# Cross-attention output projection in three fp32r products, with a single load buffer for the rows and a merge ahead

## The reference

```python
attn = jnp.einsum('bhts,bshk->bthk', probs, v)
out = jnp.einsum('bthk,hkd->btd', attn, Wo) + bo      # Wo: (16, 64, 512)
...
x = x + _L0_xattn_ref(_layernorm(x, axis=-1), ctx_1024, ctx_1024, ...)
```

## Time and profile before

| | |
|---|---|
| three timed runs | 3259.77, 3262.93, 3263.29 us (median 3262.93) |
| profiled execution | 3259.59 us, its span 3257.8 us |
| mean granted TensorE clock | 0.94 |
| busy: PE, VectorE, ScalarE, GpSimd | 3059.9, 1683.3, 1445.1, 115.1 us |
| L896, projection, 128 records | 592 ns each; overlapped |
| L886, bias row, 16 records | 7.8 us busy |
| L934, merge, 8 | 1.22 us each |
| L55, addition of two halves, 8 | 2.35 us each |
| DMA traffic | 253.18 MB, mean 78 GB/s |

### The profile page before, as it was taken

The page is one execution under the profiler, slowest core; times in us unless marked ns, Lnnn a source line. Parts: engine busy times, 40 slices in busy tenths (PEclk is TensorE's granted clock), DMA queues, the critical chain, the costliest instruction groups (busy, mean ns, idle before and its releaser), DMA issues. The chain is left out here.

```text
span 3257.8 us, 61769 instructions
## 1 busy us (share of the span) xinstructions
PE 3059.9 (94%) x25814; PEld 2672.7 (82%) x25814; DVE 1683.3 (52%) x2786; ACT 1445.1 (44%) x2978; POOL 115.1 (4%) x87
## 2 busy tenths in 40 slices
PE   6899999999999999999999999999989789969997
PEld 5788888888888888888888888888746689959997
DVE  5355655565565556556565655656533765530001
ACT  3355555555555555555555555555532420011111
POOL 0000000000000000000000000000040320100000
PEclk9799999999999999999999999999999855579998
DMA  7311221121122112112211211211270000217661
GB/s 310 110 51 39 75 65 44 44 75 52 39 75 65 45 47 77 46 39 77 63 45 56 78 39 48 78 41 41 51 172 1 17 33 0 96 56 282 251 227 60
DMA packets 234822, 253.18 MB, mean 78 GB/s; under 512 B 22328, under 2 KB 169944, under 8 KB 234096
## 3 DMA queue, kind: packets, MB, share of 16 engines
q1 hardware_dynamic: 233040, 241.79, 23.2%
q0 software_dynamic: 1280, 4.20, 0.4%
q10 hardware_dynamic: 288, 4.19, 0.3%
HBM read 215.42 MB, written 34.70 MB: 77 GB/s over the span
## 5 line engine op out<-in xcount | busy, mean ns | idle before, releaser
L272 PE MATMUL fills<-wv_group,ctxT_hi 128*128 128x256 f32 x4096 | 777.1, 285 | 1.3 <-DVE ctxT_lo L477 0.6
L280 PE MATMUL fills<-ctxT_hi,wk_pairs 128*128 128x512 f32 x2048 | 703.9, 405 | 0.6 <-DVE keys L492 0.6
L272 PEld LDWEIGHTS fills<-wv_group,ctxT_hi 128*128 128x128 f32 x4096 | 644.6, 189 | 24.2 <-issue 20.3
L492 DVE SCALAR_TENSOR_TENSOR keys<-fills,bk,keys 64x512 fp32r<-64x512 f32 x512 | 383.8, 750 | 407.5 <-ACT keys L409 403.8
L272 PE MATMUL fills<-wv_group,ctxT_lo 128*128 128x256 f32 x2048 | 571.9, 279 | 0.0
L409 ACT ACTIVATE keys<-fills,bk 64x512 fp32r<-64x512 f32 x512 | 349.5, 683 | 404.4 <-PE fills L280 401.1
L280 PEld LDWEIGHTS fills<-ctxT_hi,wk_pairs 128*128 128x128 f32 x2048 | 385.6, 188 | 102.9 <-issue 23.9
L280 PE MATMUL fills<-ctxT_lo,wk_pairs 128*128 128x512 f32 x1024 | 401.3, 392 | 0.0
L485 DVE TENSOR_TENSOR values<-fills,values 128x512 fp32r<-128x512 f32 x256 | 176.6, 690 | 416.7 <-ACT values L404 416.7
L272 PEld LDWEIGHTS fills<-wv_group,ctxT_lo 128*128 128x128 f32 x2048 | 387.0, 189 | 0.0
L529 DVE TENSOR_TENSOR probsT<-probsT_ps,probsT 128x512 fp32r<-128x512 f32 x504 | 348.2, 691 | 67.4 <-ACT probsT L441 58.8
(11 more groups left out here) (210 smaller groups left out, 2999.4 us busy)
## 6 DMA issues: line engine op xcount, KB each, us to landing
e_w<-in_L_ffn_W SPq DMA_DIRECT2D x64, 1024.0 KB, 8.8
ctx_stage<-in_ctx SPq DMA_DIRECT2D x128, 256.0 KB, 2.9
wv_group<-wv_split SPq DMA_DIRECT2D x64, 512.0 KB, 4.7
wk_pairs<-wk_split SPq DMA_DIRECT2D x128, 256.0 KB, 3.3
q<-q_split SPq DMA_DIRECT2D x256, 64.0 KB, 2.7
q_split<-p_qb SPq DMA_DIRECT2D x16, 512.0 KB, 3.8
o_parts<-o_half SPq DMA_DIRECT2D x128, 64.0 KB, 1.9
a_ua<-o_parts SPq DMA_DIRECT2D x32, 256.0 KB, 5.4
```

The costliest lines, as they stand in the source:

```text
L272: last = nc.tensor.matmul(pJ[:, bank[0], 256 * k:256 * k + 256], c[:, t, s:s + P], wv[:, w, t, :], start=t + n == 0, stop=t == DT - 1 and ...
L280: last = nc.tensor.matmul(pJ[:, bank[0], :], wk[:, p, w, t, :], c[:, t, 512 * j:512 * j + 512], start=t + n == 0, stop=t == DT - 1 and n == 2)
L492: last = nc.vector.scalar_tensor_tensor(out=keys[lo_rows(j), x, 512 * j:512 * j + 512], in0=pJ[DK * a:DK * a + DK, bk_, :], scalar=bk_sb[h ...
```

## The change

- Wo is split in two fp32r tiles, `a_xo_hi` and `a_xo_lo`, the second in place of `a_xo`. ScalarE copies the first part in four pieces, one ahead of each of its four steps of head 13 of the last batch; GpSimd subtracts the second in one instruction, between its additions of batches 0 and 1.
- Room for it: `a_ua` holds one batch instead of two, `a_w` two weights instead of three. SP loads batch 0 ahead of head 12's stores, batch 1 at head 13 after the addition of batch 0, batch 2 at head 14 after the addition of batch 1, each following one after the addition of the batch before it. The third weight is loaded in the projection block, after batch 3.
- The merged rows `a_oT`, fp32, lie in two buffers in memory of the later tile `s_AT`. ScalarE copies their first part (fp32r), VectorE subtracts the second (`rest`, both operands in SBUF). The value bias is split likewise.
- PE makes 24 fp32r products a batch instead of 16 fp32 records, and 24 for the bias row.
- VectorE's order is: rest b, merge b+1, residual b-1. ScalarE's is: widen 0 and 1, then for each b the copy of batch b, widen b+2, and after b = 0, 2 and 5 a weight copy. GpSimd's weights come after b = 1 and 5.

```diff
-        self.w = at("a_w", [P, 3, DT, D], 4096)
-        self.ua = at("a_ua", [P, 2, 2, XH // 2, P], 10240)
+        self.xo_lo = at("a_xo_lo", [P, XH // 2, D], 0, F32R)
+        self.xo_hi = at("a_xo_hi", [P, XH // 2, D], 4096, F32R)
+        self.w = at("a_w", [P, 2, DT, D], 8192)
+        self.ua = at("a_ua", [P, 2, XH // 2, P], 12288)
...
     def add(self, nc, pool, b):
-        pool.wait_ge(self.u_in[b % 2], 64 * (b // 2 + 1))
+        pool.wait_ge(self.u_in, 64 * (b + 1))
...
-                    for n in range(2):
-                        early.u_load(sp, o_parts, n)
+                    early.u_load(sp, o_parts, 0)
...
-                    for n in range(3):
-                        sp.dma_start(early.w[:, n, :, :], aw[n].rearrange("(t p) d -> p t d", p=P)).then_inc(early.w_in, 16)
-                if i >= 2:
-                    sp.wait_ge(early.added, i - 1)
+                    for n in range(2):
+                        early.w_load(sp, aw, n)
+                if i in (1, 2):
+                    sp.wait_ge(early.added, i)
...
-            for b in range(2):
-                early.add(nc, pool, b)
+            early.add(nc, pool, 0)
+            pool.wait_ge(early.xo_split, 4)
+            nc.gpsimd.tensor_tensor(early.xo_lo[:, :, :], early.xo[:, :, :], early.xo_hi[:, :, :].bitcast(F32),
+                                    ALU.subtract).then_inc(early.xo_rest, 1)
+            early.add(nc, pool, 1)
...
+                            if not more and i == 1:
+                                act.wait_ge(early.xo_in, 16)
+                                nc.scalar.copy(early.xo_hi[:, 2 * j:2 * j + 2, :], early.xo[:, 2 * j:2 * j + 2, :]
+                                               ).then_inc(early.xo_split, 1)
...
-                    for b in range(4, B):
-
-                        sp.wait_ge(early.added, b - 1)
+                    for b in range(3, B):
+
+                        sp.wait_ge(early.added, b)
                         early.u_load(sp, o_parts, b)
+                        if b == 3:
+                            sp.wait_ge(w_lo, 1)
+                            early.w_load(sp, aw, 2)
...
                         for a in range(XH // 2):
-                            last = nc.tensor.matmul(pY[:, b % 2, :], oT[:, b % 2, a, :], early.xo[:, a, :],
-                                                    start=a == 0, stop=a == XH // 2 - 1)
+                            for k, (m, w) in enumerate(((0, early.xo_hi), (0, early.xo_lo), (1, early.xo_hi))):
+                                last = nc.tensor.matmul(pY[:, b % 2, :], oT_p[:, b % 2, m, a, :], w[:, a, :],
+                                                        start=a + k == 0, stop=a == XH // 2 - 1 and k == 2)
...
-                        if b in (1, 3):
-                            weights_lo((b + 1) // 2)
+                        if b in (1, 5):
+                            weights_lo(1 + b // 4)
...
+                    def rest(b):
+                        dve.wait_ge(oT_hi, b + 1)
+                        if b >= 2:
+                            dve.wait_ge(projected, b - 1)
+                        nc.vector.tensor_tensor(oT_p[:, b % 2, 1, :, :], oT[:, b % 2, :, :], oT_p[:, b % 2, 0, :, :].bitcast(F32),
+                                                ALU.subtract).then_inc(oT_lo, 1)
...
+                    merge(0)
+                    for b in range(B):
+                        rest(b)
+                        if b + 1 < B:
+                            merge(b + 1)
...
+                    widen(0)
+                    widen(1)
+                    for b in range(B):
+                        act.wait_ge(merged, b + 1)
+                        if b >= 2:
+                            act.wait_ge(projected, b - 1)
+                        nc.scalar.copy(oT_p[:, b % 2, 0, :, :], oT[:, b % 2, :, :]).then_inc(oT_hi, 1)
+                        if b + 2 < B:
+                            widen(b + 2)
+                        if b in (0, 2, 5):
+                            n = b // 2
+                            act.wait_ge(early.w_in[n % 2], 16 * (n // 2) + 16)
+                            nc.scalar.copy(w_p[:, n, 0, :, :], early.w[:, n % 2, :, :]).then_inc(w_hi, 1)
```

More of the change, by code:

```diff
@@ L42, in __init__ @@
         self.xbv = left("a_xbv", [P, XH // 2])
-        self.xo_in, self.rs_in, self.w_in, self.added = (sem(n) for n in ("a_xo_in", "a_rs_in", "a_w_in", "a_added"))
-        self.u_in = [sem("a_u_in0"), sem("a_u_in1")]
+        self.xo_in, self.xbv_in, self.rs_in, self.added = (sem(n) for n in ("a_xo_in", "a_xbv_in", "a_rs_in", "a_added"))
+        self.xo_split, self.xo_rest, self.u_in = sem("a_xo_split"), sem("a_xo_rest"), sem("a_u_in")
+        self.w_in = [sem("a_w_in0"), sem("a_w_in1")]
     def u_load(self, sp, o_parts, b):
@@ L794, with self_attention @@
 ITERS = 20
[L797 removed]
+def self_attention(nc, x, x_bo, o_parts, row_scale, early, shared_space, aw, bq, bk, bv, wo, bo, ident, x1, route, wg, b1, b2, buf,
                    weights, first_weights, used):
@@ L835, in self_attention @@
             with ExitStack() as s1:
-                oT = sb("a_oT", [P, 2, XH // 2, P], F32, s1)
+                oT = AT[:, 0:XH, :].rearrange("p (b a) t -> p b a t", b=2)
+                oT_p = sb("a_oTp", [P, 2, 2, XH // 2, P], F32R, s1)
+                xbv_p = sb("a_xbvp", [P, 2, XH // 2], F32R, s1)
                 rsx = sb("a_rsx", [P, XH // 2, P], F32, s1)
@@ L928, in residual, with merge @@
                         norm_steps(nc, dve, step, x1, stats, mv, b)
-                    for b in range(B):
+                    def rest(b):
[4 more added lines that the diff above has]
+                                                ALU.subtract).then_inc(oT_lo, 1)
+                    dve.wait_ge(xbv_hi, 1)
+                    nc.vector.tensor_tensor(xbv_p[:, 1, :], early.xbv[:, :], xbv_p[:, 0, :].bitcast(F32),
+                                            ALU.subtract).then_inc(xbv_lo, 1)
+                    def merge(b):
                         dve.wait_ge(early.added, b + 1)
@@ L950, in _, with widen @@
                 def _(act):
-                    for b in range(B):
+                    def widen(b):
                         act.wait_ge(early.rs_in, 16 if b < B - 1 else 32)
@@ L956, in _ @@
                                        early.rs[:, b, :].unsqueeze(2).to_broadcast([P, XH, DK])).then_inc(widened, 1)
-                        if b in (0, 2, 4):
-                            act.wait_ge(early.w_in, 48)
-                            nc.scalar.copy(w_p[:, b // 2, 0, :, :], early.w[:, b // 2, :, :]).then_inc(w_hi, 1)
+                    act.wait_ge(early.xbv_in, 16)
+                    nc.scalar.copy(xbv_p[:, 0, :], early.xbv[:, :]).then_inc(xbv_hi, 1)
+                    widen(0)
[11 more added lines that the diff above has]
+                            nc.scalar.copy(w_p[:, n, 0, :, :], early.w[:, n % 2, :, :]).then_inc(w_hi, 1)
                     act.wait_ge(var_ready, 1)
```

26 lines of the change are left out of this document (15 added, 11 removed).

## The result

The changed kernel is slower: 3280.8 us at the median (3278.9 to 3282.1), the kernel before 3262.4 us (3259.8 to 3263.3), ratio 1.0058 with a 95% interval of 1.0046 to 1.0071. The forecast was 3278.0 us.

What follows compares the result with a forecast made beforehand. PE was taken to bound the projection block before, chained loads and additions after. +15.0 us there and +1.6 us in the last cross-attention group, on 3261.4, gave 3278.0 us; own case 3273 to 3282, 8-in-10 range 3269 to 3285.

Steps and rivals of the forecast that it cites:

- The chain of load and addition: Projection block: with one load buffer each load waits for the previous addition; cycle 10.07 us, five loads 50.3 us.
- This is the step that decides.: Projection block: shrinking `a_ua` from two batches to one, giving a 10.07 us cycle against 6.7 us of PE.
- The sum: Whole kernel: +15.0 us in the projection block and +1.6 us in the last cross-attention group, +16.6 us on 3261.4.
- When the addition of batch 2 ends.: Projection block start: late first weight copy and `weights_lo(0)` start the chain 10.7 us later; addition ends at 21.6 us.
- The locking out.: GpSimd instructions hold up VectorE's two-SBUF-operand ones: subtractions of batches 1, 3, 7 take 3 to 5 us, not 1.2.
- rival 1: No locking out, subtractions slip beside GpSimd: block +11.0, last group -1.6, sum +9.4 us, 3270.8 us; chance 0.15.
- PE's products.: Projection block: 24 fp32r products at 0.241 us take 5.8 us, 1.07 less per batch, 0.9 less for bias row.
- The clock at batch 7.: Projection block's end: after idling, PE runs 3.4 us at the lower clock, losing 1.7 us (bounds 0 and 2.9).
- The last group.: Last cross-attention group: GpSimd's 8.9 us Wo subtraction stalls head 13's addition, replacing a store stall; +1.6 us.
- 2 (PE remains the bound, faster): Projection block: loads land within 4.3 us, PE stays the bound; gain 9.5 less 1.6, 3253.5 us; chance 0.05.
- 3 (the clock stays low): Projection block: idling keeps PE's clock low, batches about 13.3 us; two of five make +6, 3284 us; chance 0.13.
- 4: Loads chained but cheaper, for instance by a sooner first weight copy: +4 to +7, 3266 to 3268 us; chance 0.05.

Runs made afterwards that it cites:

- e1: Changed kernel with a second load buffer for odd batches from 3 on; 3261.11 us, ratio 1.000 to the kernel before.
- e4: Kernel before the change with `a_ua` halved to one batch and the matching waits, products still fp32; 3255.81 us, ratio 0.9984.
- e6: Changed kernel, single load buffer kept, batch 2 added before any weight subtraction, third weight loaded later, Wo's second part in four pieces; 3259.67 us, one execution.
- e5: Changed kernel with Wo's second part subtracted in four GpSimd pieces and batch 1's addition held until head 13's addition; 3277.86 us, one execution.
- e2: Changed kernel with GpSimd's third weight subtraction moved from after batch 5's to after batch 7's bias addition; 3278.42 us, one execution.
- e8: Changed kernel with one of the three products left out, for the batches and the bias row; 3269.28 us, one execution.
- e10: Same as e9, plus 56 unused 32x32 transposes at the end of PE's projection block; 3249.14 us, ratio 0.9966 to the kernel before.
- e9: Same as e7, but the third weight is loaded after batch 5 instead of batch 4; 3252.50 us, ratio 0.9977 to the kernel before.
- e3: Changed kernel with GpSimd adding batch 2 before the first weight subtraction; 3280.43 us, one execution.
- e7: Same as e6, but with the second load buffer of e1; 3258.94 us, ratio 0.999 to the kernel before.

## Why the prediction was right, and where it was not

**The chain of load and addition.** Right in mechanism and size. A cycle of 10.07 us was put together from 7.65 and 2.35; the additions came 9.8 to 10.6 us apart. e1 takes the chain away by one buffer, and 21.2 us go.

**"This is the step that decides."** Too simple. e4 has the same buffer and the same 10 us steps and loses nothing, for PE needs 7.74 us a batch there and the chain starts at 9.7 us instead of 21.6. What decides is the buffer together with the late start and with products cheap enough to wait. e6 has the buffer and the cheap products, starts early, and keeps 1.8 of the 15.4 us. The sum had all three in it; the sentence named one.

**When the addition of batch 2 ends.** Forecast 21.6 us after the first copy, measured 21.6. The parts agree as well: `weights_lo(0)` at 13.6 forecast and 13.7 measured, the subtraction of batch 1 at 14.6 (2410.96 is 14.6).

**The locking out.** Right at all three places named: 4.75, 3.77 and 3.77 us at batches 1, 3 and 7. The rows of before had shown the pattern on other pairs of instructions only the earlier trace rows; rival 1, that it wouldn't happen to this one, fell, and e5 and e2 show the same from the other side. (The Trainium skill, SBUF — State Buffer, section Who interferes with whom, calls the shared ports an exclusive lock; the 6.18 us of an addition of 0.29 agree.) The lock also works in GpSimd's disfavour: its addition of batch 2 is 3.38 us long instead of 2.35, as it waits for VectorE's subtraction. The sum had this case (19.3 for the subtraction's end, 21.6 for the addition's).

**PE's products.** 0.241 us each by rows 3, measured 0.234. PE waited for 19.3 us in the block, so this had no weight. e8, with a third of the products gone, shortened the block by only 3.4 us: the addition of batch 2 ended 2.3 us sooner, the bias row ahead of it being shorter, and from the last subtraction to the residual of batch 7 it took 1.3 us less.

**The clock at batch 7.** Charged with 1.7 us, measured 2.1 to 2.3: 7.9 us instead of 5.6 to 5.8 for 24 products. It came back 5 us after work resumed, 3.4 in the row I had used.

**The end of the block.** 86.8 forecast, 87.2 measured.

**The last group.** +1.6 forecast. From GpSimd's first addition to the block's start it was 39.0 us before and 40.6 after, +1.7. That the two agree so well is partly luck: the forecast had its 1.6 us at the maximum of head 15, where 1.0 was measured, and nothing behind it, where 0.7 was. The exchange of a stall of 6.12 us (a store) for one of 6.18 us (the lock) is as described, and e5 shows that without either the block starts 4.3 us sooner.

**The sum.** +16.6 forecast, +19.4 in the spans (+18.4 by the medians, with the median of before 1.0 us above the 3261.4 from which the forecast counted). Of the missing 2.8 us 2.7 are the loop of sums, which the prediction counted at nothing without saying so: the diff doesn't touch it. e8 and e10 put it on the position in PE's instruction stream. That such code can change its time isn't to be seen in any row of before.

**The rivals.** 2 (PE remains the bound, faster) failed by its own condition: the load lands in 7.6 us, 4.3 were needed. Yet its price for the block was about right: it gave 9.5 us, and with the loads off the chain, in e9, the block is 10.7 us shorter than before. 3 (the clock stays low) came half: the clock fell in three of the waits, ahead of batches 3, 5 and 7, and each time was back after some 3 to 5 us of work. Batches 3 and 5 were slower by it, and the load cycle of 10 us hid that, as the argument against the rival had it; only batch 7 paid. 4 needed a sooner first weight copy; it came when forecast.

## What to carry to other kernels

Before a buffer is given up for room, write the cycle that it creates (transfer, plus the work that frees it) beside the time of the engine that should be the bound, and count from when the cycle starts: a cycle of 10 us was free at a start of 9.7 us and cost 15 us at 21.6 us with a faster PE. When a wait is moved, read on in the order of every queue behind it; e3 and e7 each lost their gain to the next instruction of the same queue. A long GpSimd instruction with two SBUF operands belongs where VectorE has none of that kind, or in pieces behind a wait.

## What the runs showed of the hardware beyond that

- A loop on PE, with the same instructions and the same granted clock (0.50), takes 199.3 to 199.8 or 202.0 to 202.3 us depending on how many PE instructions stand ahead of it (+0 and +256: short; +144: long). Nothing in between was seen in twelve kernels.
- The lock between VectorE and GpSimd goes both ways, and which of the two comes first within 0.7 us decided over 3.2 us (1.82 or 5.00 for the same subtraction). VectorE, once it waits, comes ahead of GpSimd's next instruction: in e2 ahead of `weights_lo(2)` (5.57 instead of 4.5 us), in the changed kernel ahead of the addition of batch 2 (3.38 instead of 2.35).
- One fp32 product of 128x512 took 0.86 us of PE, three fp32r products 0.70 us, so the split in three is 19% cheaper on PE, for 1.04 us of ScalarE and 1.22 us of VectorE per batch, and once, for Wo, four copies of 1.05 us on ScalarE and 8.88 us on GpSimd.
